# First expert layer's norm, gate, ranking and row scatter inside the attention iterations, one row for both choices

## The chip, the cores and the metric

One core of one Trainium2 chip. The metric is device time in microseconds (us) of one execution. The core has five engines with queues of their own: TensorE (PE in the profile, its weight loads PEld), VectorE (DVE), ScalarE (ACT), GpSimd (POOL) and SyncE (SP, which here only issues DMAs). Each works its queue in order; they meet through semaphores.

## The reference, cut to what matters

32 batches of 256 tokens with 128 channels go through two layers. The change touches the first, attention and a mixture of experts, both behind a norm that a condition vector scales and shifts:

```python
h = layernorm(x) * (1 + scale_a) + shift_a
c_k = h @ w_dk + b_dk; k = c_k @ w_uk + b_uk          # v likewise; q = h
q, k = rope(q), rope(k)                               # 16 heads of 8
x = x + gate_a * (softmax(q k^T / sqrt(8)) v @ w_o + b_o)

h = layernorm(x) * (1 + scale_b) + shift_b            # what is moved
logits = h @ gate_w                                   # [tokens, 8]
top_vals, top_idx = top_k(logits, 2)
mult1 = softmax over experts not masked by (thr - logits) / max(|logits|, thr) > 0.02, at top_idx[0]
mult2 = the same for the second choice, the first set to -inf
y = sum over the 8 experts of w_e * ((silu(h @ w1[e]) * (h @ w3[e])) @ w2[e])
x = x + gate_b * y
```

Each token goes to two of eight experts. The second layer (a Mamba mixer in both directions, a Fourier KAN and a one-choice mixture) follows and is not changed.

## The kernel before, in words

X, the residual, stays in SBUF: 64 tiles of 128 tokens, two per batch (TC = 2). The program is a row of stages; in each, every engine has its code written out in full, and waits on semaphores order them.

`load_and_modulate` loads constants and X. `attention` (from line 358) is one software pipeline over i = 0 to 37, unrolled. Iteration i handles six batches at different ages: projections and rotary sum of batch i, its load from DRAM in split bf16 parts (i+1), row maxima of the scores (lag MAX = 2), their transpose (ROWS = 3), scores, exponentials and values (AV = 4), sums and transposes (OUT = 5), bias, gate and residual update (LAST = 6). TensorE runs eight slots per iteration (`slot`), each with two row-maximum products (L632), one score product pair (L645) and one value product (L659); small steps stand between the slots, and all of these write the one PSUM bank `PP` (a_proj). VectorE runs 16 row maxima per iteration (`row_max`, L566) from a buffer two deep, with the other steps between them by hand; TensorE waits for the maximum before last. ScalarE runs eight exponentials (L483). GpSimd runs the gate product and update (L446, L450), the cosine product (L454), and two of the rotary split steps (L458, L461). SP stores the split parts and loads Q and K.

After the loop `norm_stats` finishes mean and deviation for all 64 tiles, `pad_rows` makes the filler rows, and `ffn_front` (line 764) runs alone: ScalarE normalises (L841) and copies each row a second time for its second choice (L835 also serves that copy and the transposed tile), VectorE modulates (L944, L946), TensorE turns (L899) and gates (L885), and VectorE routes groups of eight tiles (`route`): two times maximum, equality, rank by expert (L950 to L954), limits, weights, and slots from counts that TensorE sums with a triangular matrix and one of ones (L891, L892). GpSimd sends each row of 130 numbers (128 channels, destination row, weight) to its slot in DRAM by an indirect DMA of 128 rows: 64 tiles x 2 choices = 128 scatters (L913). At the end VectorE writes the table of expert and first row for 71 tiles of 256 slots (L1037 to L1054), and SP stores a filler block behind each expert's rows, at an address loaded from `pad_row` (L829, L830).

`experts0` (line 1057) then takes 71 tiles: SP loads rows (L1091) and weights (L1092) by the table, TensorE turns (L1112) and multiplies (L1135, L1139, L1122), VectorE takes index and weight from the row (L1175, L1176), GpSimd scatters the result (L1185).

Of the kernel before, what the change touches and what calls it, by code (L numbers as in the profile page):

```python
# [13 lines left out]
P = 128  # L14
# [122 lines left out]
def load_and_modulate(core, first):  # L137
# [3 lines left out]
    for n, shape, dt in (("bias_kv", [P, 2], F32), ("bias_cols", [P, 4], F32), ("bias_out", [P, TC * D], F32), ("bias_out_row", [1, D], F32),  # L141
                         ("b_o_row", [1, D], F32), ("ones_row", [1, P], F32), ("cos", [P, 2 * T], F32), ("sin", [P, 2 * T], F32),
                         ("minus_one", [2, H * T], BF16)):
        kept[n] = core.sbuf("a_" + n, shape, dt, on=first)
# [5 lines left out]
    w_dk, w_dv, w_uk, w_uv, w_uvg, w_o, rot, w_k, w_v, bias_kv, bias, bo, bo_row, bo_in, ones1, cos, sin, minus = (kept[n] for n in (  # L150
        "w_dk", "w_dv", "w_uk", "w_uv", "w_uv_by_group", "w_o", "rot", "w_k", "w_v", "bias_kv", "bias_cols", "bias_out", "bias_out_row", "b_o_row",
        "ones_row", "cos", "sin", "minus_one"))
    on = ExitStack()
    with on:
        c = core.sbuf("c_rows", [2 * B, D], on=on)
# [141 lines left out]
def ln_finish(core, tag, st, eps, block):  # L297

    nc = core.nc
    m, dm, v, sd = core.ln_tmp  # L300
    s_v, s_sd = core.sem(f"{tag}_var_ready"), core.sem(f"{tag}_std_ready")

    @block.vector
    def _(dve):
        chain = Chain(core, dve, f"{tag}_dve_chain")

        chain.step(nc.vector.tensor_tensor(m[:], st[:, :, 1], st[:, :, 4], ALU.add))
        nc.vector.tensor_tensor(dm[:], st[:, :, 1], st[:, :, 4], ALU.subtract)
        chain.step(nc.vector.tensor_tensor(v[:], st[:, :, 2], st[:, :, 5], ALU.add))
        chain.step(nc.vector.tensor_tensor(dm[:], dm[:], dm[:], ALU.mult))  # L310
        chain.step(nc.vector.tensor_scalar(dm[:], dm[:], 0.25, eps, ALU.mult, ALU.add))
        nc.vector.scalar_tensor_tensor(out=v[:], in0=v[:], scalar=1.0 / D, in1=dm[:],
                                       op0=ALU.mult, op1=ALU.add).then_inc(s_v, 1)
        dve.wait_ge(s_sd, 1)
        chain.step(nc.vector.reciprocal(core.rstd[:], sd[:]))
        chain.step(nc.vector.scalar_tensor_tensor(out=core.nmr[:], in0=m[:], scalar=-0.5, in1=core.rstd[:],
                                                  op0=ALU.mult, op1=ALU.mult))

    @block.scalar
    def _(act):  # L320
        act.wait_ge(s_v, 1)
        nc.scalar.activation(sd[:], v[:], ACT.Sqrt).then_inc(s_sd, 1)


# [5 lines left out]
def norm_stats(core, tag, eps=LN_EPS):  # L330

    with core.nc.Block() as block:
        ln_finish(core, tag, core.st, eps, block)

PAIRS = H // 2
# [22 lines left out]
def attention(core, kept):  # L358
    nc, B, X, aps = core.nc, core.B, core.X, core.aps
# [7 lines left out]
    valued = lambda p: ((p - 7) % PAIRS, ROWS if p == 7 else AV)  # L367
    on = ExitStack()
    with on:
# [17 lines left out]
        y1, y2 = sb("y1", [P, TC * D]), sb("y2", [P, TC * D])  # L387
        ST = core.psum("a_scores", [P, 2, 2, TC, T], on=on)
# [10 lines left out]
            "y_ps", "y_biased", "y_gated", "x_updated", "stats")}  # L399
        loaded = [core.sem(f"a_loaded{n}") for n in range(RING)]  # L400

        with nc.Block() as block:
            @block.sync
            def _(sp):
# [3 lines left out]
                for i in range(B + LAST):  # L408
# [16 lines left out]
                    if live(i, 1):  # L425
# [4 lines left out]
                        for turn in range(PARTS):  # L430
# [3 lines left out]
                            if turn:  # L434
                                sp.dma_start(K9[n][first + cut:past, :, :].rearrange("p h t -> p (h t)"), rows[1, 0:turn * DH]).then_inc(loaded[n], 16)

            @block.gpsimd
            def _(pool):
                for i in range(B + LAST):
                    if live(i, LAST):  # L440
# [9 lines left out]
                        nc.gpsimd.tensor_tensor(x, x, y2[:], ALU.add).then_inc(S["x_updated"], 1)  # L450
# [296 lines left out]


GT = 8
NB = GT // TC  # L750
PADROW = 1.0e6


# [2412 lines left out]
```

## Time and profile before

| | us |
|---|---|
| timed runs, median of 3 | 3265.21 (3264.02 to 3269.38) |
| profiled execution, span from first to last instruction (the profile gives no other time of it) | 3315.9 |
| attention, first instruction to last residual update | 0 to 617.8 |
| stage of norm, gate, ranking, scatter | 617.8 to 852.2 |
| first experts, from their first matmul | 852.2 to 1245 |

| of the span | TensorE | VectorE | ScalarE | GpSimd |
|---|---|---|---|---|
| busy us | 2742.9 | 2509.0 | 2252.2 | 2145.6 |

Busy shares over the whole span mix stages with different limits. A stage is read from the windows: which engine is busy all the time there, at which granted TensorE clock (1.00 is 2.4 GHz, 0.5 is 1.2 GHz), and what the others wait for. In timelines the bracket at the end of a row is the idle time of that engine before it, and what ended it.

### The profile page before, as it was taken

What the parts mean: (1) busy time and instruction counts of PE and PEld (TensorE: products, weight loads), DVE (VectorE), ACT (ScalarE), POOL (GpSimd) and SP (SyncE); (2) the same over time, 40 slices, a digit from 0 to 9 for tenths busy, and PEclk for the clock granted to TensorE, in tenths of its full rate; (3) what the DMA queues carried; (4) which work ended last, traced back from release to release, by engine and by line L of the source; (5) the groups of instructions that cost most, each with busy time, mean ns of one, the idle gap of its engine ahead of it and who ended that gap; (6) DMA issues with size and microseconds to landing.
All of it is one profiled execution on the core that took longest, in us unless ns stands there. A gap on an engine that the chain in (4) does not pass through costs nothing. (4 is left out here: it accounts for less than half of the span.)

```text
span 3315.9 us, 55572 instructions
## 1 busy us (share of the span) xinstructions
PE 2742.9 (83%) x18699; PEld 2096.9 (63%) x18699; DVE 2509.0 (76%) x3291; ACT 2252.2 (68%) x4086; POOL 2145.6 (65%) x1488
## 2 busy tenths in 40 slices
PE   6999999522699996788888888989888887769983
PEld 3555555311699993466666666666666666669983
DVE  5788887434233334699999999999999999967993
ACT  2677776511222224999999999999999999656651
POOL 2233332266233334899999999999999999743574
PEclk6999998655899998899999999999999999889996
DMA  5555554211566666222222222222222222322322
GB/s 134 99 102 102 101 101 82 60 58 51 160 190 193 193 178 209 81 78 78 77 73 85 80 81 80 83 74 76 84 81 80 83 77 75 102 55 72 81 73 53
DMA packets 202783, 321.54 MB, mean 97 GB/s; under 512 B 37418, under 2 KB 109638, under 8 KB 197898
## 3 DMA queue, kind: packets, MB, share of 16 engines
q1 hardware_dynamic: 189282, 299.01, 32.8%
q0 software_dynamic: 12224, 18.29, 1.6%
q8 instruction: 160, 2.62, 0.3%
q14 instruction: 109, 0.89, 0.1%
q10 hardware_dynamic: 1008, 0.72, 0.1%
HBM read 269.84 MB, written 55.68 MB: 98 GB/s over the span
## 5 line engine op out<-in xcount | busy, mean ns | idle before, releaser
L1702 POOL TENSOR_TENSOR resid_x<-s_ux,s_B_rows 128x1024 f32<-128x1024 f32 x256 | 605.3, 2364 | 85.6 <-PE s_y L2432 84.5
L2263 DVE TENSOR_TENSOR_SCAN resid_x<-s_dA,resid_x 128x1024 f32<-128x1024 f32 x256 | 581.8, 2273 | 28.9 <-ACT s_dA L1914 22.6
L2271 DVE TENSOR_TENSOR_SCAN resid_x<-s_late,s_back_in 128x1024 f32<-128x1024 f32 x256 | 583.4, 2279 | 20.8 <-ACT s_late L1924 16.4
L2432 PE MATMUL s_y<-identity,resid_x 128*128 128x128 f32 x4096 | 552.4, 279 | 10.5 <-issue 8.4
L2432 PEld LDWEIGHTS s_y<-identity,resid_x 128*128 128x128 f32 x4096 | 493.3, 145 | 65.1 <-issue 38.9
L1710 POOL TENSOR_TENSOR resid_x<-resid_x,s_C_rows 128x1024 f32<-128x1024 f32 x192 | 453.7, 2363 | 0.2 <-DVE resid_x L2263 0.2
L566 DVE TENSOR_REDUCE a_row_max<-a_maxscores 128x2 f32<-128x512 f32 x512 | 336.3, 684 | 89.2 <-PE a_maxscores L632 88.7
L2278 DVE TENSOR_TENSOR resid_x<-resid_x,s_C 128x1024 f32<-128x1024 f32 x320 | 382.1, 1194 | 5.5 <-PE s_C L2407 5.5
L1914 ACT ACTIVATE s_dA<-s_dt,s_A 128x510 f32<-128x510 f32 x512 | 330.0, 676 | 67.7 <-DVE resid_x L2263 66.5
L2419 PE MATMUL s_back_in<-identity,resid_x 128*128 128x128 f32 x2048 | 291.4, 288 | 101.3 <-ACT resid_x L1935 53.0
L1924 ACT ACTIVATE s_late<-s_dt,s_A 128x510 f32<-128x510 f32 x512 | 338.0, 710 | 0.0
L2419 PEld LDWEIGHTS s_back_in<-identity,resid_x 128*128 128x128 f32 x2048 | 239.1, 147 | 143.9 <-issue 79.1
L483 ACT ACTIVATE a_probs<-a_scores 128x1024 f32<-128x1024 f32 x256 | 262.1, 1024 | 94.7 <-PE a_scores L645 88.3
L1185 POOL DMA_INDIRECT choice_outputs<-e_y,e_idx x142 | 137.8, 971 | 273.3 <-DVE e_y L1176 249.4
L1169 DVE TENSOR_TENSOR e_g<-e_silu,e_ps 128x512 f32<-128x512 f32 x142 | 97.7, 688 | 283.4 <-PE e_ps L1139 282.2
L1158 ACT ACTIVATE e_silu<-e_ps 128x512 f32<-128x512 f32 x142 | 84.8, 597 | 242.1 <-PE e_ps L1135 240.1
L2990 PE MATMUL k_psY<-k_coef_T,k_basis 128*128 128x128 f32 x2048 | 235.5, 277 | 6.7 <-ACT k_basis L2953 4.3
L2990 PEld LDWEIGHTS k_psY<-k_coef_T,k_basis 128*128 128x128 f32 x2048 | 232.8, 194 | 7.5 <-DVE k_basis L2881 4.7
L632 PE MATMUL a_maxscores<-a_K,a_Q 72*128 72x256 bf16 x1024 | 207.8, 287 | 15.6 <-DMA a_K<-split_qk 11.3
L2459 PE MATMUL s_prep<-s_xT,k_coef_T 128*128 128x512 f32 x464 | 210.9, 596 | 2.7 <-ACT s_xT L2012 1.6
L2407 PE MATMUL s_C<-s_bc_parts,s_w_sel 96*128 96x512 bf16 x320 | 125.9, 393 | 88.5 <-DVE resid_x L2278 88.5
L913 POOL DMA_INDIRECT slot_inputs<-choice_rows,f_slots x128 | 125.9, 983 | 95.5 <-DVE f_slots L1009 57.8
(463 smaller groups left out, 5643.8 us busy)
## 6 DMA issues: line engine op xcount, KB each, us to landing
s_B_rows<-forward_rows SPq DMA_DIRECT2D x256, 256.0 KB, 3.2
e_w<-L_ffn_w_by_expert SPq DMA_DIRECT2D x71, 768.0 KB, 4.6
s_C_rows<-forward_rows SPq DMA_DIRECT2D x192, 256.0 KB, 3.3
a_Q<-split_qk SPq DMA_DIRECT2D x96, 192.0 KB
split_qk<-a_parts SPq DMA_DIRECT2D x32, 384.0 KB, 2.8
e_x<-slot_inputs SPq DMA_DIRECT2D x71, 130.0 KB
a_K<-split_qk SPq DMA_DIRECT2D x64, 128.0 KB
s_late<-choice_outputs SPq DMA_DIRECT2D x16, 512.0 KB, 4.6
```

Source lines behind the costliest of these rows:

```text
L483: nc.scalar.activation(PT[:, q % 4].rearrange("p a b t -> p (a b t)"), ST[:, q % 2].rearrange("p a b t -> p (a b t)"), ACT.Exp, scale=SCAL ...
L566: nc.vector.tensor_reduce(mx[b % 2][:, h, :], MX[:, h % 2], AX.X, ALU.max).then_inc(S["max_done"], 1)
L1702: tt(R[s, 0], ux[par][:], brow[s % BRING][:].unsqueeze(1).broadcast_to([P, C2, W]), ALU.mult).then_inc(S["in_ready"], 1)
L1710: tt(r, r, crow[k % CRING][:].unsqueeze(1).broadcast_to([P, C2, W]), ALU.mult).then_inc(S["part_pool"], 1)
L1914: last = func(dA[:, c2, :, 1:T], dt[par][:, 0, c2, :].rearrange("p (g t) -> p g t", t=T)[:, :, 1:T], ACT.Exp, scale=Wt["A"][:, 0, c2, s:s ...
L1924: last = func(dec[s % 2][:, c2, :, 0:T - 1], dt[par][:, 1, c2, :].rearrange("p (g t) -> p g t", t=T)[:, :, 0:T - 1], ACT.Exp, scale=Wt["A" ...
L2263: nc.vector.tensor_tensor_scan(r, a, r, 0.0, ALU.mult, ALU.add).then_inc(S["scanned"], 1)
L2271: nc.vector.tensor_tensor_scan(r[:, ::-1], a[:, ::-1], b[:, ::-1], 0.0, ALU.mult, ALU.add).then_inc(S["scanned"], 1)
L2278: tt(r, r, CP[:].unsqueeze(1).broadcast_to([P, C2, W]), ALU.mult).then_inc(S["part_dve"], 1)
L2419: last = nc.tensor.transpose(bP[:, c2, k // TC, (k % TC) * P:(k % TC + 1) * P], bt[s % 2][:, k, c2 * P:(c2 + 1) * P], core.ident[:])
L2432: last = mm(YP[:, t, c2 * P:(c2 + 1) * P], R[s, d][:, c2, t * P:(t + 1) * P], core.ident[:], is_transpose=True, start=((s, d) == (0, 1) an ...
L2990: last = mm(psY[:, j % 2, k * D:(k + 1) * D], basis[j % 2][:, m, k * P:(k + 1) * P], WT[:, m, :], start=(m == EARLY[0] and k == 0), stop=( ...
```

## The change

1. `ffn_front`, `norm_stats`, `ln_finish` and `pad_rows` go. `FrontPlan` lays their steps into the attention's turns: groups of four batches (five of them) and then of two (six); a batch's norm stands at least seven turns behind its last attention input; choice and ranking one and two turns after the group's last norm; scatters four per turn up to turn 31 or 32, then all that are open. The loop gets 43 turns instead of 38.
2. By FrontPlan for 32 batches: one norm per turn in turns 11 to 31 (batches 0 to 20), two in 32, 33, 35, 37 and 39, one in 34; choices in turns 15, 19, 23, 27, 31, 33, 34, 35, 36, 38, 40; rankings in 16, 20, 24, 28, 32, 34, 35, 36, 37, 39, 41; scatters: 4 in each of turns 17 to 32, 16 in 33, 8 in each of 35, 36, 37, 38, 40, 42.
3. The variance (seven small operations) and the modulation move to GpSimd, the root becomes Ln and Exp on ScalarE, the norm stays on ScalarE. Transposes, gate products and counts use free columns of `PP`. The counts become bf16 and add up over the group's tiles in PSUM (1 + 8 matmuls for eight tiles).
4. One row of 132 numbers serves both choices: it holds token row, both weights, and the rank of the first expert; both scatters of a tile read it. `experts0` finds by that rank which choice a row is (`code_of_tile`) and forms index and weight in five small VectorE operations per tile.
5. The tables are made by 16 operations on all partitions at the end of the loop. The rotary sum stays on VectorE.

```diff
+        for b in range(B):
+            i = max(self.groups[self.group_of[b]][1] + last + 1, self.norm_at[b - 1] if b else 0)
+            while held.get(i, 0) >= (2 if i >= B else 1):
+                i += 1
+            self.norm_at[b] = i
...
+                def modulate(b):
+                    g = plan.group_of[b]
...
+                    pool.wait_ge(S["f_xn"], b + 1)
+                    pool.wait_ge(S[f"f_mod_loaded{b % 2}"], 16 * (b // 2 + 1))
...
+                    gtt(h, h, row(1), ALU.mult).then_inc(S["f_scaled"], 1)
...
+                    gtt(h, h, row(0), ALU.add).then_inc(S["h_ready"], 1)
...
+                    if i in plan.root_at:
+                        offset(plan.root_at[i])
+                    if plan.early(i) is not None:
+                        modulate(plan.early(i))
+                    if plan.late(i) is not None:
+                        modulate(plan.late(i))
+                    sent, due = plan.scattered_by.get(i - 1, 0), plan.scattered_by[i]
+                    scatters(sent, (sent + due) // 2)
                     if live(i, 0):
                         pool.wait_ge(S["k_ready"], i + 1)
                         at(pool, S["roped_ready"], i)
                         nc.gpsimd.tensor_tensor(qcos[:], qk[:].rearrange("p a t -> p (a t)"), cos[:], ALU.mult).then_inc(S["cos_done"], 1)
+                    scatters((sent + due) // 2, due)
...
+                    if i in plan.rank_at:
+                        places(plan.rank_at[i])
+                    if plan.late(i - 1) is not None:
+                        logits_kept(i, plan.late(i - 1))
+                    row_max(i, 2)
+                    row_max(i, 3)
+                    if i in plan.rank_at:
+                        distances(plan.rank_at[i])
+                    row_max(i, 4)
+                    if i in plan.rank_at:
+                        slot_rows(plan.rank_at[i])
+                    row_max(i, 5)
+                    if i in plan.rank_at:
+                        limits(plan.rank_at[i])
...
+                    if i in plan.rank_at:
+                        weights(plan.rank_at[i])
...
                     row_max(i, 10)
+                    if i in plan.choose_at:
+                        first_choice(plan.choose_at[i])
                     row_max(i, 11)
...
                     row_max(i, 13)
+                    if i in plan.choose_at:
+                        second_choice(plan.choose_at[i])
...
+                    for k in range(TC):
+                        last = nc.tensor.transpose(PP[:, T + k * P:T + (k + 1) * P], Hrow[g % HRING][:, n + k, 0:D], core.ident[:])
...
+                    for k in range(TC):
+                        last = mm(PP[:, T + k * E:T + (k + 1) * E], hT[:, k, :], gw[:], start=True, stop=True)
...
+                    mm(PP[:, P:P + n * E], tri[:], flat, start=True, stop=False, skip_group_check=True)
+                    for j in range(1, n + 1):
+                        last = mm(PP[:, P + j * E:P + (n + 1) * E], allone[:], flat[:, 0:(n + 1 - j) * E], start=False, stop=(j == n), skip_group_check=True)
...
                     slot(i, 6)
...
+                    if plan.late(i) is not None:
+                        second_turn(i, plan.late(i))
```

In a norm's turn ScalarE runs the two norms after exponential 0 and the copy of the turned tiles before exponential 7; the gate product of that batch comes at the start of the next turn, after slot 0. In `experts0` the wait for earlier stores of a buffer moves half a tile forward, from the output product to the index.

## Rows read from the trace of the kernel before

**Rows 1.** Windows by stage: busy us (count) per engine, clock, DMA share, GB/s
```profile
335.00:536.00 201.00, 198.93 (x1831) 118.54 (x1826) 163.71 (x307) 148.74 (x220) 61.21 (x62) 1.00 0.53 102
562.00:590.00 28.00, 27.16 (x152) 12.97 (x153) 13.04 (x23) 10.18 (x11) 2.19 (x4) 0.52 0.02 4
852.00:1245.00 393.00, 390.69 (x2411) 356.70 (x2412) 125.97 (x282) 113.26 (x214) 133.94 (x138) 0.99 0.61 189
```
**Rows 2.** Instruction groups, the scatters: line, engine, operation, shapes, count, busy us, mean, idle
```profile
L913 POOL DMA_INDIRECT slot_inputs<-choice_rows,f_slots x128 | 125.9, 983 | 95.5 <-DVE f_slots L1009 57.8 <-issue 32.3 <-DMA slot_inputs<-choice_rows,f_slots 5.5
```
**Rows 3.** Timeline of GpSimd, one iteration: start, us, engine, line, operation, idle before
```profile
350.73 0.73 POOL L446 TENSOR_TENSOR a_y<-a_y,a_gate_rows 128x256 f32<-128x256 f32 x1 [1.22 <-DVE a_y L573]
356.77 1.28 POOL L454 TENSOR_TENSOR a_qk_cos<-a_qk,a_cos 128x512 f32<-128x512 f32 x1 [4.52 <-ACT a_qk L498]
362.23 1.15 POOL L458 TENSOR_TENSOR a_left<-a_roped,a_parts 128x512 f32<-128x512 f32 x1 [4.18 <-DVE a_roped L596]
364.75 1.16 POOL L461 TENSOR_TENSOR a_parts<-a_left,a_parts 128x512 bf16<-128x512 f32 x1 [1.37 <-ACT a_parts L519]
367.13 0.73 POOL L446 TENSOR_TENSOR a_y<-a_y,a_gate_rows 128x256 f32<-128x256 f32 x1 [1.22 <-DVE a_y L573]
```
**Rows 4.** Timeline of GpSimd, gate products and last update
```profile
547.59 0.73 POOL L446 TENSOR_TENSOR a_y<-a_y,a_gate_rows 128x256 f32<-128x256 f32 x1 [1.22 <-DVE a_y L573]
561.40 0.72 POOL L446 TENSOR_TENSOR a_y<-a_y,a_gate_rows 128x256 f32<-128x256 f32 x1 [12.29 <-DVE a_y L573]
588.58 0.73 POOL L446 TENSOR_TENSOR a_y<-a_y,a_gate_rows 128x256 f32<-128x256 f32 x1 [25.65 <-DVE a_y L573]
616.23 0.72 POOL L446 TENSOR_TENSOR a_y<-a_y,a_gate_rows 128x256 f32<-128x256 f32 x1 [4.21 <-DVE a_y L573]
617.03 0.72 POOL L450 TENSOR_TENSOR resid_x<-resid_x,a_y 128x256 f32<-128x256 f32 x1
```
**Rows 5.** Timeline of TensorE in iteration 350.73
```profile
353.23 0.44 PE L684 MATMUL a_proj<-identity,a_xn 128*128 128x128 f32 x2
353.50 0.38 PE L632 MATMUL a_maxscores<-a_K,a_Q 72*128 72x256 bf16 x2
355.58 0.61 PE L691 MATMUL a_proj<-a_w_v,a_qk 128*128 128x128 f32 x4
356.02 0.38 PE L632 MATMUL a_maxscores<-a_K,a_Q 72*128 72x256 bf16 x2
```
**Rows 6.** Timeline of VectorE, the end of that iteration
```profile
363.27 2.60 DVE L566 TENSOR_REDUCE a_row_max<-a_maxscores 128x2 f32<-128x512 f32 x4
366.63 0.43 DVE L573 TENSOR_TENSOR a_y<-a_proj,a_bias_out 128x256 f32<-128x256 f32 x1 [0.76 <-PE a_proj L720]
```
**Rows 7.** Timeline of VectorE in the ranking of the old stage
```profile
640.00 0.22 DVE L953 TENSOR_REDUCE f_rank<-f_cand 128x8 f32<-128x64 f32 x1
640.25 0.22 DVE L954 TENSOR_TENSOR f_choice<-f_cand,f_rank 128x64 f32<-128x64 f32 x1
```
**Rows 8.** Timeline of TensorE at the start of iteration 33
```profile
562.84 0.39 PE L632 MATMUL a_maxscores<-a_K,a_Q 72*128 72x256 bf16 x2 [1.98 <-DMA a_K<-split_qk]
```
**Rows 9.** Timeline of ScalarE in the old stage
```profile
632.90 0.37 ACT L835 ACTIVATE f_hT<-f_psT 128x256 f32<-128x256 f32 x1
633.16 0.87 ACT L841 ACTIVATE f_xn<-resid_x,neg_mean_rstd,rstd 128x128 f32<-128x128 f32 x2
```
**Rows 10.** Timelines and waits at the end of the old stage
```profile
838.19 0.97 POOL L913 DMA_INDIRECT slot_inputs<-choice_rows,f_slots  x1 [0.30 <-issue]
...
812.54 33.39 SPq L830 DMA_DIRECT2D slot_inputs<-f_pad_rows  x8
849.97 0.37 SPq L1091 DMA_DIRECT2D e_x<-slot_inputs  x1
...
SPq L801 <- DMA slot_inputs<-f_pad_rows: 2.0, 1, 2.0
...
852.16 0.69 PE L1112 MATMUL e_psX<-identity,e_x 128*128 128x128 f32 x2 [45.57 <-DMA e_x<-slot_inputs]
```

More of the change, by code:

```diff
@@ L294, in load_and_modulate @@
     return kept
[L297 to L322, printed above, removed]
@@ L325, in tile_stats, with region @@
 def tile_stats(core, src, tile):
     return core.nc.vector.bn_stats(core.st[:, ds(tile, 1), :].rearrange("p n k -> p (n k)"), src[:, ds(tile * D, D)])
-def norm_stats(core, tag, eps=LN_EPS):
-    with core.nc.Block() as block:
-        ln_finish(core, tag, core.st, eps, block)
 PAIRS = H // 2
+E, F = 8, 512
+FC = F // P
+STAGES = 4
+CAP = 80
+ROWS0 = 2
+TOK = ROWS0 * P
+GT = 8
+NB = GT // TC
+PADROW = 1.0e6
+HRING = 4
+ROW_TOK, ROW_W, ROW_RANK = D, D + 1, D + 3
+def region(core):
+    return core.NT * P + TOK
@@ L440, in _ @@
+                nc.gpsimd.memset(allone[:], 1.0)
+                nc.gpsimd.memset(pad[:], 0.0).then_inc(S["f_pad"], 1)
+                pool.wait_ge(S["f_pad"], 1)
+                nc.gpsimd.memset(pad[:, :, ROW_TOK], PADROW).then_inc(S["f_pad"], 1)
+                for i in range(plan.turns):
                     if live(i, LAST):
@@ L569, in _ @@
+                front_constants()
+                for i in range(plan.turns):
                     if live(i, LAST):
@@ L668, in slot @@
                     values(i, p)
-                for i in range(B + LAST):
+                for i in range(plan.turns):
+                    turned = max((b for b in plan.norm_at if plan.norm_at[b] < i), default=-1) + 1
+                    ranked = sum(1 for turn in plan.rank_at if turn <= i)
                     slot(i, 0)
+                    if plan.late(i - 1) is not None:
+                        logits(i, plan.late(i - 1))
+                    if i in plan.rank_at:
+                        counts(i, plan.rank_at[i])
                     if live(i, ROWS):
@@ L3093, in adaln_two_layers @@
     with core.stack:
+        XS, tables, tiles = choice_buffers(core)
         first = ExitStack()
         with first:
-            attention(core, load_and_modulate(core, first))
+            attention(core, load_and_modulate(core, first), XS, tables, tiles)
         late = ExitStack()
         with late:
-            YS, kept = ffn0(core, late)
+            YS, kept = ffn0(core, late, XS, tables, tiles)
             core.next_stage()
```

647 lines of the change are left out of this document (325 added, 322 removed).

## The prediction

> **What bounds the kernel now.** I read the windows by stage first, then the timelines of single engines. In a steady attention iteration (335 to 536) TensorE is busy 198.9 of 201.0 us at clock 1.00 while VectorE has 163.7, ScalarE 148.7 and GpSimd 61.2 [rows 1]: TensorE's instruction count sets the 16.40 us of an iteration (367.13 less 350.73 [rows 3]). The expert layer's norm, gate and scatter stand alone after it. The last attention update starts at 617.03 and takes 0.72 us [rows 4], so X is final at 617.75; the first expert matmul starts at 852.16 [rows 10]. That is 234.4 us with TensorE almost empty. Of it GpSimd issues 128 scatters, 125.9 us busy at 983 ns each [rows 2], and with the 0.30 us between two the pitch is 1.27 us: 163 us. So the stage is bound by GpSimd's issue of scatters, and behind it is a tail: last scatter ends 839.16, first expert load issues 849.97, first matmul 852.16 [rows 10]. From 852 on TensorE is again full, 390.7 of 393 us [rows 1].
>
> **What the change does to the end of the chain.** The stage goes; 64 scatters fall into turns 17 to 32 (4 in each), where GpSimd has 11 us free per iteration, and 64 into turns 33 to 42 (16, then 8 in each of six). So the new end is: attention up to turn 32, slower by what is added; then GpSimd's serial work from turn 33; then the old tail.
>
> *Attention, turns 11 to 31.* One batch per turn adds two transposes and two gate matmuls. A pair of such transposes advances TensorE 0.27 us (353.23 to 353.50), four f32 records with 128x128 weights 0.44 us (355.58 to 356.02) [rows 5]. 21 x 0.27 + 20 x 0.44 = 14.5 us, all on the bound engine. Counts: nine bf16 matmuls per group; the trace has no such row. From above 0.11 us each, the average over the 1831 records of 335 to 536 [rows 1], so 1.0 us; from below nothing. I take 0.6, since the columns are 64 at most: four groups, 2.4 us.
>
> *VectorE.* The ranking is cut in small operations, each awaited: pitch 0.26 us at 128x64 (640.00 to 640.25 [rows 7]). A turn that chooses gets twelve, 1.55 us between row maxima 10 and 11 and 1.55 between 13 and 14. That is where VectorE has no room: four row maxima stand back to back at 0.65 us from 363.27 to 365.87, and the only gap is the 0.76 us before 366.63 [rows 6]. TensorE's score buffer is two deep, so it stands still: about 1.2 us at the first insertion and 0.45 at the second after the added TensorE work is set against it, 1.65 in all. A turn that ranks gets twelve operations plus the logits copy, 3.4 us, but most in the first half, where there is slack; only the three before row maximum 10 hit the tight part. I take 0.9 us. From below both are zero (the 0.7 us that TensorE is longer gives VectorE room), from above the whole 3.1 and 3.4 us. Five choosing turns and four ranking turns before turn 32: 8.3 + 3.6 = 11.9 us (0 to 29).
>
> *ScalarE* gets two norms (0.87 us for the pair) and one copy (0.37 us) [rows 9] per turn, beside 52 us idle in 201 [rows 1], so 4.2 us free per iteration: covered; without the cover 1.2 us a turn, 26 us. *GpSimd*: an iteration has 0.73 + 0.72 + 1.28 + 1.15 + 1.16 = 5.0 us [rows 3]; modulating adds two of 0.73 and scatters 4 x 1.27, 11.6 us of 17.1. The halves fit the gaps: gap to the cosine product 4.5 us (modulate, two scatters: 4.0, though it waits for the norm first, perhaps 0.5 late), gap to L458 4.2 us (two scatters: 2.5). Behind GpSimd's scatter waits only the rotary chain, whose sum is needed 2 us later. Its statistics (seven small operations of about 0.2 us) come after L461 and before the next gate product; the update they delay is read 5 us later. SP gets one 128 KB load a turn behind the K/Q loads: covered, since it is last in the queue.
>
> Turn 32 began on GpSimd at 547.59 [rows 4]; now 547.6 + 14.5 + 2.4 + 11.9 = 576.4.
>
> *Turn 32 and 33.* Turn 32 took 561.40 - 547.59 = 13.8 us [rows 4]; it gets two turns of rows, two logits, counts and a ranking: + 3.0, so turn 33 starts at 593.2. Turn 33 before lasted 27.2 us (588.58 less 561.40). It starts with TensorE's 1.98 us wait for a K load [rows 8], and the window 562 to 590 has clock 0.52 [rows 1]. With turn 32 longer by 3 us that wait should go, and turn 33 should take about 14 + 2.5.
>
> *GpSimd serial from 593.2.* Turn 33: gate 1.5, two modulates 3.1, 16 scatters 20.4, statistics 2: to 620.2. Turn 34: VectorE's bn_stats stand before the row sums and wait for GpSimd's update, 620.2 + 1.5; then statistics 0.5, choice 1.3, division and product 0.8 (VectorE), transposes, copy, projection and bias 2.5: about 628. Turn 35: 1.5 + 3.1 + 8 scatters 10.2 + 2, to 645. Turn 36: 1.5 + 10.2, to 656.9. Turn 37: 1.5 + 3.1 + 10.2 + 2, to 673.7. Turn 38: root on ScalarE 1, 10.2, to 685. Turn 39: two modulates, 688.3. Turn 40: 698.5. Turn 42: 708.7. The last group's own chain (turn, gate, two choices, counts, places, weights) runs on VectorE beside turn 40 and ends near 697.5; the 16 operations for the tables then need some 7 us, to 704.5, and are hidden. Add 2.0 us for the last write to land (as the pad writes: 2.0), and 849.97 - 847.9 + 2.2 = 4.3 for block end, register loads and first load [rows 10]: first expert matmul at 715.
>
> 852.2 - 715 = 137 us of the profiled span. Two corrections. The eight pad stores, with the register loads between them, took 33.4 us (812.54 on [rows 10]) while scatters ran; the span is 3315.9 us against the 3265.2 of the timed runs, so stretches like this may be the profile's. Without it the old stage ends with the scatters, 839.2 + 2 + 4.3 = 845.5, and the saving is 130. And I allow 7 us for late K loads, since traffic rises and a single load already was late once. Saving 123 to 124.
>
> The experts get five VectorE operations of 128x2 per tile (0.17 us each at most) on an engine busy 126 of 393 us [rows 1]: nothing; without cover 71 x 0.8 = 57 us. Rows are 528 instead of 520 bytes: nothing. The write wait is now for the tile three before instead of four; those scatters lie two tiles (11 us) back.
>
> **Rivals.**
> *Clock lost in a few turns.* Speaks for it: one wait of 1.98 us was followed by 27 us at 1.2 GHz, although TensorE was then busy 27.16 of 28 us [rows 1, 8]: at the lower level this loop doesn't win the clock back by itself. My choosing turns have stalls of 1.2 us. Against: the rows show no case between an undisturbed iteration and the 1.98 us, so I can't place the point; and transposes and gate matmuls are added. Each loss costs 27.2 - 13.8 = 13.4 us: one to five of them, 3155 to 3208.
> The Trainium skill, page TensorE: Matmul & The Clock Gate (Part 1: The HAM clock gate), says that the throttled state is the default and recent activity releases it. The trace agrees that the lower level follows a stretch with little work, and differs in the return: TensorE was dense for 27 us and stayed at 1.2 GHz. If activity released it at once, a loss would cost a few us instead of the 13.4 that the row gives, and the sum would be 3141 with or without losses.
> *The clock lost for good, slower than before.* The same, but from turn 15 to 31: an iteration of 16.4 + 0.7 us becomes twice (27.2 / 13.8 = 1.97) as long, + 16.6 us each, 17 turns 282 us, less the 12 us of stalls that then hide: 3141 + 270 = 3411. It decides the sign from 124 / 16.6 = 7.5 such turns on.
> *Scatters don't fit between GpSimd's rotary steps.* Each turn with scatters would be longer by up to 4 x 1.27 = 5.1 us, 16 turns: + 82, 3223. For: the first gap is 4.5 us and 4.0 plus a wait for ScalarE goes in. Against: the product has 2 us of slack.
> *VectorE absorbs all and the waits in turn 34 vanish.* 12 + 8 + 7 us better: 3114.
>
> **How the numbers follow.** Forecast 0.60; a few clock losses 0.20; scatters don't fit 0.09; absorbed 0.06; clock lost for good 0.05. Time 3265.2 - 124 = 3141 us. Range 3112 to 3200: it takes in the absorbed case, the upper bound of the VectorE stalls (+17), uncovered K loads, and the cases of one to four clock losses; above it are the fifth loss, most of the misfit case and the last rival. A run can't tell less than 0.2% (6.5 us) from no change. Faster 0.94, same 0.01, slower 0.05.
>
> **What would show it.** Distance of two GpSimd gate products: about 17.1 us in plain turns, 18 to 19 in turns 19, 20, 23, 24; first e_psX matmul near 715; TensorE waits on row maxima of about 1.2 us in choosing turns; no K wait in turn 33 and clock 1.00 until about 610; scatters back to back at 1.27 us from turn 33. Wrong would be: a clock of 0.5 in the loop, GpSimd's cosine product later than 2 us, or a stage between the last scatter and the experts longer than 10 us.

## The result, and the profile after

| | us |
|---|---|
| timed runs, changed kernel, median of 4 | 3225.89 (3214.50 to 3238.96) |
| the kernel before beside them, median of 4 | 3267.14 (3264.02 to 3269.38) |
| ratio | 0.9864, 95% interval 0.9829 to 0.9899 |
| profiled execution: span / its own time | 3221.9 / 3223.75 |
| first expert matmul | 761.7 (before 852.2) |

The kernel is 41 us faster, a third of the 124 us predicted, and outside the range of 3112 to 3200 us. Each of the two kernels was profiled again, unchanged, and the comparison below needs these profiles too.

**The loop.** Windows of the changed kernel: turns 15 and 16 (the first that chooses and the first that ranks), a plain turn, turn 33, what follows it, and the experts; the last figures are the granted clock, DMA share and GB/s. They answer to [rows 1].

```profile
core 0: us, PE busy (x) PEld busy (x) DVE busy (x) ACT busy (x) POOL busy (x), PEclk, DMA share, GB/s
270.00:291.00 21.00, 19.03 (x152) 11.26 (x145) 16.48 (x39) 13.21 (x21) 6.35 (x9) 0.86 0.47 96
291.00:314.00 23.00, 22.59 (x168) 13.09 (x167) 15.84 (x39) 13.37 (x22) 6.34 (x8) 0.76 0.41 64
331.00:348.00 17.00, 17.00 (x159) 10.45 (x158) 13.34 (x26) 13.47 (x23) 10.87 (x13) 1.00 0.60 119
624.00:652.00 28.00, 19.27 (x197) 11.33 (x194) 16.76 (x50) 12.78 (x20) 21.80 (x31) 0.91 0.17 53
652.00:762.00 110.00, 42.67 (x235) 23.00 (x235) 34.32 (x164) 23.89 (x48) 66.81 (x90) 0.50 0.16 50
762.00:1155.00 393.00, 390.68 (x2414) 357.28 (x2412) 159.23 (x567) 113.26 (x214) 134.02 (x138) 0.99 0.62 190
```

A plain turn is full and at 1.00. The choosing turn has TensorE 19.0 of 21 us busy, and the clock is down to 0.86 in it and to 0.76 in the next one, where TensorE is busy 22.6 of 23 us for work that fits in 17.5 at full clock. The predicted sign of a wrong forecast, "a clock of 0.5 in the loop", is there: TensorE runs at 1.2 GHz for 17.1 us from 285.1, and again from 363.6, 445.6, 524.1 and 602.6, once in each of the five choosing turns. Just ahead of every one stands the same row, here TensorE in turns 15 and 23 (the bracket is the idle time before the row and what ended it; it answers to [rows 5]):

```profile
284.35 0.39 PE L970 MATMUL a_maxscores<-a_K,a_Q 72*128 72x256 bf16 x2 [1.97 <-DVE a_row_max L770]
...
444.15 0.39 PE L970 MATMUL a_maxscores<-a_K,a_Q 72*128 72x256 bf16 x2 [1.97 <-DVE a_row_max L770]
```

**VectorE and GpSimd ahead of that wait** (timelines of turn 15; before, this place looked as in [rows 6]):

```profile
280.63 0.69 DVE L770 TENSOR_REDUCE a_row_max<-a_maxscores 128x2 f32<-128x512 f32 x1
281.23 0.21 DVE L802 TENSOR_REDUCE a_top<-a_biased 128x8 f32<-128x64 f32 x1
281.48 0.23 DVE L803 TENSOR_TENSOR a_is_max<-a_biased,a_top 128x64 f32<-128x64 f32 x1
281.74 1.06 DVE L804 TENSOR_TENSOR a_cand<-a_is_max,a_rev 128x64 f32<-128x64 f32 x1
282.83 0.22 DVE L805 TENSOR_REDUCE a_choice_rows<-a_cand 128x8 f32<-128x64 f32 x1
283.09 0.23 DVE L806 TENSOR_TENSOR a_choice<-a_cand,a_choice_rows 128x64 f32<-128x64 f32 x1
283.35 0.23 DVE L807 SCALAR_TENSOR_TENSOR a_biased<-a_choice,a_biased 128x64 f32<-128x64 f32 x1
283.61 0.69 DVE L770 TENSOR_REDUCE a_row_max<-a_maxscores 128x2 f32<-128x512 f32 x1
```

```profile
281.51 1.20 POOL L613 TENSOR_TENSOR a_left<-a_roped,a_parts 128x512 f32<-128x512 f32 x1 [4.18 <-DVE a_roped L926]
```

The six operations of the first choice were to take 1.55 us between the row maxima. They take 2.38, and the surplus is one operation: L804, 1.06 us where its neighbours of 128x64 take 0.23. It begins after GpSimd's difference L613 (281.51 to 282.71) and ends just behind it, at 282.80.

**The drain.** GpSimd in turns 33 to 35 and at the end, TensorE's first expert row, and all scatters as one group (these answer to [rows 2, 3, 10]):

```profile
629.69 1.04 POOL L575 DMA_INDIRECT slot_inputs<-a_choice_rows,a_slots  x1 [0.16 <-POOL a_choice_rows L563]
...
648.92 0.97 POOL L575 DMA_INDIRECT slot_inputs<-a_choice_rows,a_slots  x1 [0.30 <-issue]
...
651.54 0.72 POOL L591 TENSOR_TENSOR a_y<-a_y,a_gate_rows 128x256 f32<-128x256 f32 x1
...
653.98 0.72 POOL L563 TENSOR_TENSOR a_choice_rows<-a_choice_rows,a_mod_rows_b 128x256 f32<-128x256 f32 x1
667.00 0.73 POOL L591 TENSOR_TENSOR a_y<-a_y,a_gate_rows 128x256 f32<-128x256 f32 x1 [12.30 <-DVE a_y L889]
```

```profile
752.29 0.97 POOL L575 DMA_INDIRECT slot_inputs<-a_choice_rows,a_slots  x1 [0.30 <-issue]
```

```profile
761.66 0.69 PE L1193 MATMUL e_psX<-identity,e_x 128*128 128x128 f32 x2 [27.11 <-DMA e_x<-slot_inputs]
```

```profile
L575 POOL DMA_INDIRECT slot_inputs<-a_choice_rows,a_slots x128 | 127.7, 998 | 40.5 <-issue 36.9 <-DVE a_choice_rows L856 2.6 <-POOL a_choice_rows L563 0.9
```

Turn 33 (gate product to gate product) is 27.05 us, as predicted: its 16 scatters follow each other at 1.27 us. Then GpSimd stands idle for 12.3 us, until VectorE's bias step for the next update is done. VectorE had itself stood for 9.37 us behind GpSimd's update L595, which follows the scatters:

```profile
653.16 0.49 DVE L299 BATCH_NORM_STATS2 bn_stats<-resid_x 128x6 f32<-128x128 f32 x2 [9.37 <-POOL resid_x L595]
```

From 646.9 us on TensorE runs at 1.2 GHz for the whole rest of the drain. In the second profile of the changed kernel (e11 below) it runs so for 13.7 us from 638.5 and then at 2.4 GHz for 17 us, and there GpSimd's wait in turn 34 is 9.60 us (e11):

```profile
656.41 0.73 POOL L591 TENSOR_TENSOR a_y<-a_y,a_gate_rows 128x256 f32<-128x256 f32 x1 [9.60 <-DVE a_y L889]
```

**The kernel before, profiled twice more** (c0 and c1 below). Windows of c0: turn 33 and the old stage; under it the same two stretches of c1.

```profile
558.00:574.00 16.00, 14.55 (x147) 8.64 (x151) 12.65 (x24) 9.03 (x11) 1.46 (x3) 1.00 0.03 8
602.00:803.00 201.00, 48.91 (x224) 45.19 (x224) 95.91 (x433) 50.38 (x139) 126.42 (x128) 0.50 0.26 76
```

```profile
561.00:588.00 27.00, 25.07 (x147) 12.52 (x151) 13.35 (x24) 9.16 (x10) 1.79 (x3) 0.57 0.02 5
616.00:817.00 201.00, 48.91 (x224) 45.18 (x224) 95.92 (x433) 50.38 (x139) 126.49 (x129) 0.50 0.25 76
```

The stage that I had priced at 234.4 us is 201 in both, with equal busy times. The first expert matmul is at 803.2 and 817.3, not 852.2. In the first profile GpSimd had three gaps that the others do not have (8.97, 10.10 and 9.96 us; the first is shown, from the kernel before). And SP's eight pad stores took 8.18 us in c1 instead of 33.39 [rows 10]; from the end of the last scatter to the issue of the first expert load it was 10.8 us in the first profile and 5.3 us in c0 and c1.

```profile
696.54 1.17 POOL L913 DMA_INDIRECT slot_inputs<-choice_rows,f_slots  x1 [8.97 <-DVE f_slots L1009]
```

```profile
736.31 8.18 SPq L830 DMA_DIRECT2D slot_inputs<-f_pad_rows  x8
```

### The profile page after: what moved, and what is told of

Same layout as the page of the kernel before. It is cut to its first block and busy times, and to the rows that moved or that the text cites. A ratio compares the mean times of both kernels' runs of the same rounds, so it can differ in the third digit from the quotient of the medians.

```text
span 3221.9 us, 56259 instructions
## 1 busy us (share of the span) xinstructions
PE 2767.1 (86%) x18742; PEld 2103.5 (65%) x18742; DVE 2513.1 (78%) x3462; ACT 2241.6 (70%) x4076; POOL 2212.7 (69%) x1654
## 5 line engine op out<-in xcount | busy, mean ns | idle before, releaser
L2508 PE MATMUL s_y<-identity,resid_x 128*128 128x128 f32 x4096 | 560.6, 282 | 11.7 <-issue 10.5
L2508 PEld LDWEIGHTS s_y<-identity,resid_x 128*128 128x128 f32 x4096 | 500.5, 147 | 68.1 <-issue 43.2
L2011 ACT ACTIVATE resid_x<-s_uT,s_bT 128x256 f32<-128x256 f32 x432 | 185.3, 498 | 0.8
```

Source lines behind the costliest of these rows:

```text
L2508: last = mm(YP[:, t, c2 * P:(c2 + 1) * P], R[s, d][:, c2, t * P:(t + 1) * P], core.ident[:], is_transpose=True, start=((s, d) == (0, 1) an ...
```

## Experiments

Times are compared through the ratio to the kernel before on the same chip, where there is one.

**c0_before_again, c1_before_again: the kernel before, unchanged.**

> The kernel before, unchanged, profiled once more. Its first profile spans 3315.9 us against 3265 in timed runs, and it shows two things that need not repeat: 27.3 us of half clock from 563 and 31 us of SyncE and VectorE issuing one instruction per 0.7 to 1.4 us from 812 on. Theory A (the profile's own disturbance): the span falls to within 15 us of 3267 and at least one of the two is gone. Rival (both belong to the kernel): span again above 3300 with both.

> The kernel before once more, unchanged. The first profile had a stage of 234 us between attention and experts and a turn 33 of 27.2 us, the second 201 us and 15.7 us. If the first was disturbed in the stage, this one has 200 to 205 us there; turn 33 may be either (the wait for the K load was 1.98 us where the clock fell and 1.74 us where it stayed).

3262.12 and 3281.77 us, first expert matmul 803.2 and 817.3. The stage is 201.2 and 201.3 us. Turn 33 is 15.7 us in c0 and 26.2 in c1, and this is what lies ahead of it on TensorE (c0, then c1):

```profile
559.45 0.39 PE L632 MATMUL a_maxscores<-a_K,a_Q 72*128 72x256 bf16 x2 [1.74 <-DMA a_K<-split_qk]
```

```profile
562.93 0.39 PE L632 MATMUL a_maxscores<-a_K,a_Q 72*128 72x256 bf16 x2 [2.04 <-DMA a_K<-split_qk]
```

So the first profile was longer by 33 us in the stage, by 11.5 in turn 33 compared with c0, and by 3.3 ahead of turn 6. The stage's 33 us are in neither of the other two executions; turn 33's clock is lost in c1 as it was in the first. What made the stage longer stays open.

**e1_spread: the changed kernel, its choices cut up.** In turns before 34 the twelve choice operations go one to three at a time behind row maxima 3, 5, 6, 7, 9, 11, 13, 15, and the last three of a ranking go behind 9, 10, 11.

```diff
+AFTER = {3: 1, 5: 3, 6: 1, 7: 2, 9: 1, 11: 1, 13: 1, 15: 2}
...
 row_max(i, 10)
-first_choice(plan.choose_at[i])       # six awaited operations
 row_max(i, 11)
+take(choosing, AFTER[11])             # one
```

> The changed kernel with the twelve operations of both choices laid singly or in pairs and threes into VectorE's gaps between row maxima (1 after maximum 3, 3 after 5, 1 after 6, 2 after 7, 1 after 9, 11 and 13, 2 after 15) in turns 15, 19, 23, 27, 31 and 33, and the three weight operations after 9, 10, 11. Theory (TensorE's stall of over 1 us costs the clock): no half clock in turns 15 to 32, those turn pairs fall from 44 to 47 us to about 36, turn 32 starts near 570 instead of 608, time about 3187 (3175 to 3200). Rival 1 (the clock falls for the number of VectorE operations or the DMA load, not for the stall's length): clock losses stay, within 8 us of 3226. Rival 2 (gain is eaten by GpSimd in the drain): turn 32 starts near 570, but the first expert matmul moves less than 15 us.

3181.16 us (3178.35 to 3183.01), ratio 0.9721 (0.9697 to 0.9744). Windows of turns 15 and 16, and TensorE's longest wait in them:

```profile
270.00:289.00 19.00, 17.70 (x166) 10.33 (x164) 17.43 (x40) 13.75 (x22) 7.11 (x9) 1.00 0.57 112
289.00:306.00 17.00, 16.91 (x163) 10.16 (x156) 14.99 (x38) 12.97 (x22) 5.97 (x8) 1.00 0.51 92
```

```profile
285.04 0.44 PE L1052 MATMUL a_proj<-identity,a_choice_rows 128*128 128x128 f32 x2 [0.66 <-DVE a_out_rows L987]
```

No clock is lost in turns 6 to 32; the first expert matmul is at 717.7. Theory and size hold: this placement alone is worth 44 us at the first expert matmul. TensorE's wait in the other four choosing turns is 0.67 us. The hold behind GpSimd's difference is not gone: the third choice operation, L823 at 283.22, still takes 0.92 us. But it now stands alone, and TensorE waits 0.66 us for it instead of 1.97 for all six.

**e3_filler: the changed kernel, with TensorE kept busy.** VectorE's work stays as it is; TensorE repeats score products (same result) in slots 6 and 7 of choosing turns.

```diff
+for turn in range(1 + extra):         # extra: 2 in slot 6, 1 in slot 7
     for j, h in enumerate(pair_heads(q)):
```

> The changed kernel with added work: in the choosing turns TensorE repeats the score product of slot 6 twice and that of slot 7 once (same values written again), so that it works where it stood still for VectorE. Theory (the clock falls because TensorE does too little in the stall): although 12 matmuls per choosing turn are added, no half clock in turns 15 to 31, pairs of turns about 37.5 us, time 3190 to 3205. Rival (lost time is the stall itself, or the clock falls for another reason): time 3226 or up to 7 us more, half clock as before.

3200.53 us (3187.87 to 3213.24), ratio 0.9792 (0.9752 to 0.9831). The longest wait is 1.10 us, the clock falls in one of the five turns (I had expected none), and turn 15 takes 19.7 us instead of 21.3. VectorE's operations are all still there, and yet the first expert matmul is at 726.3, 35 of e1's 44 us earlier; by the ratios it is 24 of 47 us, the runs falling into two groups (3187.9 to 3190.1 and 3211.0 to 3213.2). So half of the loss or more was the clock and not VectorE's time.

**e4_stall_before: the kernel before, with the stall alone.** Six awaited operations of 128x64 on a scratch tile at the two places, in turns 15, 19, 23, 27, 31.

```diff
 row_max(i, 10)
+if i in (15, 19, 23, 27, 31): idle_ops()   # a fill and five products
 row_max(i, 11)
```

> The kernel before with nothing of the change but six awaited operations on a small scratch tile (128x64) on VectorE after row maxima 10 and 13 of turns 15, 19, 23, 27 and 31. Theory (a stall of 1.2 us is enough to lose the clock, and in this loop it comes back only after 17 to 24 us): five stretches at half clock, about 8 to 10 us each: 3267 + 40 to 55 us = 3307 to 3322. Rival (a stall costs its own length): 1.65 to 3.1 us each, 3275 to 3283, clock 1.00 from 120 to 540.

3323.45 us (3312.05 to 3333.53), ratio 1.0143 (1.0110 to 1.0175): 51 us slower than the kernel before on the same chip, within the 40 to 55 expected. VectorE, GpSimd and TensorE in turn 15:

```profile
280.36 2.10 DVE L558 TENSOR_TENSOR a_dummy<-a_dummy 128x64 f32<-128x64 f32 x5
...
285.21 1.26 DVE L558 TENSOR_TENSOR a_dummy<-a_dummy 128x64 f32<-128x64 f32 x5
```

```profile
280.44 1.15 POOL L458 TENSOR_TENSOR a_left<-a_roped,a_parts 128x512 f32<-128x512 f32 x1 [4.18 <-DVE a_roped L603]
```

```profile
283.24 0.39 PE L643 MATMUL a_maxscores<-a_K,a_Q 72*128 72x256 bf16 x2 [1.93 <-DVE a_row_max L573]
```

Five products take 1.26 us at the second place and 2.10 at the first, where GpSimd's difference runs. All five turns lose the clock. The losses are not alike: the first four have 13.7 to 17.1 us of half clock and cost 8 to 10 us each with the wait itself, the one of turn 31 takes 61.4 us, through turns 32 and 33, which are 25.4 us each instead of the 13.8 and 15.7 of c0.

**e7_half_stall, e10_three_again, e8_stall_four, e9_stall_five: how long the wait is.** As e4, with three, three again, four and five operations.

```diff
-for _ in range(6):
+for _ in range(3):                    # e7 and e10; 4 in e8, 5 in e9
```

> The kernel before with three awaited scratch operations instead of six at each of the two places, in the same five turns (15, 19, 23, 27, 31). Theory A: the loss of the clock has a point between the stalls that kept it (1.10 us) and those that lost it (1.93 us), and this one stays below it with about 1.1 us: no half-clock stretch in those turns, choosing turns 17.2 to 17.8 us, 4 to 8 us slower than before in all. Theory B: the clock already falls at stalls of this length in this loop: choosing turns near 19 and the next near 21, 35 to 50 us slower than before.

> The kernel before with four scratch operations at each of the two places in turns 15, 19, 23, 27, 31. Three gave TensorE a wait of 1.15 us in each of the five turns, and the clock fell in two of them; six gave 1.93 us and it fell in all five. Theory A, the longer the wait the more often it falls: a wait near 1.4 us, three or four of five lost, 3295 to 3320. Theory B, the length in this range doesn't matter and other things decide (then the five of five at 1.93 us were chance): one or two lost.

> As the run before it with five scratch operations: a wait near 1.65 us. Theory A: four or five of five lost, 3305 to 3330. Theory B: again one or two.

> The kernel with three scratch operations once more, unchanged, since the same wait of 1.15 us had kept the clock in turns 15, 19 and 27 and lost it in 23 and 31. If it is a matter of chance between executions, other turns lose it now, one to three of five; if something in turns 23 and 31 decides, the same two: 3295 to 3312 either way.

| | wait in each of the five turns, us | turns that lost the clock | time, us |
|---|---|---|---|
| e7 | 1.15 | 2 (23, 31) | 3303.06 (3300.65 to 3311.74), ratio 1.0097 (1.0066 to 1.0128) |
| e10 | 1.15 | 2 (19, 27) | 3293.16, one run |
| e8 | 1.41 | 3 | 3315.65, one run |
| e9 | 1.67 | 5 | 3331.76, one run |
| e4 | 1.93 | 5 | 3323.45 |

e7's TensorE in turn 19, which kept the clock, and in turn 23, which lost it, and the windows of turns 16 and 24 behind such waits:

```profile
347.05 0.39 PE L643 MATMUL a_maxscores<-a_K,a_Q 72*128 72x256 bf16 x2 [1.15 <-DVE a_row_max L573]
...
413.90 0.39 PE L643 MATMUL a_maxscores<-a_K,a_Q 72*128 72x256 bf16 x2 [1.15 <-DVE a_row_max L573]
```

```profile
284.00:301.00 17.00, 16.83 (x158) 10.01 (x157) 13.99 (x27) 12.28 (x19) 5.33 (x6) 1.00 0.48 88
419.00:441.00 22.00, 21.83 (x159) 12.16 (x161) 14.07 (x27) 12.36 (x19) 5.36 (x6) 0.76 0.35 65
```

The same wait of 1.15 us has both outcomes in one execution, and the turns change between executions. My theory of a point between 1.10 and 1.93 us, with 1.15 below it, fell with e7, which is 34 us slower than before where I had 4 to 8. Most of that is the loss at turn 31, which again took in turns 32 and 33 (58.0 us at half clock in e7, e8 and e9). e10 kept the clock in turn 31 and is 2 us below its range, and e9 is 2 us above its own. The counts 2, 2, 3, 5, 5 of five rise with the wait, but e12 below breaks the row.

**e11_after_again: the changed kernel, unchanged.**

> The changed kernel once more, unchanged. Its first profile lost the clock in all five choosing turns at a wait of 1.97 us, 9 to 10 us each. Expected again in four or five of five, 3213 to 3240, and the first expert matmul between 755 and 775 us; if the losses of the first profile were chance, one to three, 3190 to 3210 and 725 to 745 us.

3215.63 us, first expert matmul 749.4. Three turns lose the clock (15, 19, 27), as in my second case, and 23 and 31 keep it at the same wait; the time is in the range of my first case and the matmul between the two, for I had put a loss at 9 to 10 us. TensorE in turns 15 and 23, and the windows of the turns behind them:

```profile
285.82 0.39 PE L970 MATMUL a_maxscores<-a_K,a_Q 72*128 72x256 bf16 x2 [1.98 <-DVE a_row_max L770]
...
444.65 0.39 PE L970 MATMUL a_maxscores<-a_K,a_Q 72*128 72x256 bf16 x2 [1.98 <-DVE a_row_max L770]
```

```profile
292.00:316.00 24.00, 23.59 (x174) 13.62 (x176) 16.57 (x41) 13.82 (x23) 6.98 (x8) 0.75 0.40 67
450.00:467.00 17.00, 16.59 (x162) 10.25 (x155) 15.11 (x39) 12.92 (x22) 10.10 (x11) 1.00 0.56 102
```

Turns 15 and 16 take 21.1 + 23.4 us, turns 23 and 24 take 19.7 + 17.5: one loss costs 7.3 us here, 8.8 in turns 19 and 20. So the number of losses can account for a part of the spread of the changed kernel's runs, 3214.5 to 3239.0; how many losses the runs without a profile had isn't shown.

**e12_one_input, e13_left_written_only: who holds VectorE.** e12 is e4 with reductions in place of the five products. In e13, the changed kernel, GpSimd's L613 writes zeros instead of reading two tiles; this leaves out the second and third part of the rotary split, so e13 computes something else and serves as a test alone.

```diff
-tt(dummy[:], dummy[:], dummy[:], ALU.mult)                            # e4
+nc.vector.tensor_reduce(dummy2[:], dummy[:], AX.X, ALU.max)           # e12
```

```diff
-nc.gpsimd.tensor_tensor(left[:]..., roped[:]..., parts[:, :, 0, :], ALU.subtract).then_inc(S["left1"], 1)
+nc.gpsimd.memset(left[:], 0.0).then_inc(S["left1"], 1)                # e13
```

> The kernel before with the six scratch operations of e4 at the same places, but as a fill and five reductions of 128x64 to 128x8 (one input tile each) instead of products (two input reads each). In e4 the five products took 2.10 us after row maximum 10, where GpSimd's difference (128x512, 1.15 us, at 280.44) ran beside them, and 1.26 us after row maximum 13, where GpSimd was idle: 0.84 us of the 1.93 us wait. Theory A, VectorE's products and GpSimd's difference can't run at the same time and a reduction can: 1.26 us at both places, TensorE's wait near 1.1 us, two of five turns with a lost clock, 3290 to 3305. Theory B, something else holds VectorE there (the semaphore steps, the row maximum's buffer): the wait stays 1.9 us, five lost, near 3323. By the Trainium skill, page SBUF — State Buffer, a VectorE instruction with two inputs in SBUF blocks against a GpSimd instruction that reads SBUF, one with a single input does not; by that rule theory A.

> The changed kernel, in which GpSimd fills the residue of the rotary split with zeros (it writes only) in place of the difference that reads two tiles; this leaves out the second and third part of that split. Theory A: the third operation of the first choice (1.06 us at 281.74, its like 0.23) goes back to 0.23, TensorE's wait in choosing turns from 1.97 to about 1.15 us, the clock is lost in two or three of five turns, 3190 to 3212. Theory B: the operation is long for another reason, 1.97 us and four or five lost, 3214 to 3239.

VectorE, GpSimd and TensorE of e12 in turn 15 (this execution's turns start 8 us later than e4's); the last row is from turn 23:

```profile
287.87 1.24 DVE L558 TENSOR_REDUCE a_dummy<-a_dummy 128x8 f32<-128x64 f32 x5
...
291.86 1.24 DVE L558 TENSOR_REDUCE a_dummy<-a_dummy 128x8 f32<-128x64 f32 x5
```

```profile
287.96 1.16 POOL L458 TENSOR_TENSOR a_left<-a_roped,a_parts 128x512 f32<-128x512 f32 x1 [4.18 <-DVE a_roped L603]
```

```profile
289.89 0.39 PE L643 MATMUL a_maxscores<-a_K,a_Q 72*128 72x256 bf16 x2 [1.06 <-DVE a_row_max L573]
...
441.62 0.38 PE L643 MATMUL a_maxscores<-a_K,a_Q 72*128 72x256 bf16 x2 [0.49 <-DVE a_row_max L573]
```

VectorE's third operation of the first choice in e13, and TensorE's wait in turn 19:

```profile
278.36 0.22 DVE L803 TENSOR_TENSOR a_cand<-a_is_max,a_rev 128x64 f32<-128x64 f32 x1
```

```profile
350.21 0.39 PE L969 MATMUL a_maxscores<-a_K,a_Q 72*128 72x256 bf16 x2 [1.13 <-DVE a_row_max L769]
```

Both say theory A for the held operation: reductions take 1.24 us at both places though GpSimd's difference runs from 287.96 to 289.12, and the operation of 1.06 us is 0.22 once GpSimd does not read. The Trainium skill, page SBUF — State Buffer (Who interferes with whom), says that a VectorE instruction with two inputs in SBUF contends with a GpSimd instruction that reads SBUF. The trace agrees, with 0.84 us (1.06 less 0.22 in e13, 2.10 less 1.26 in e4).

On the clock they differ. e13: 3189.24 us (3184.42 to 3193.47), ratio 0.9736 (0.9663 to 0.9809), wait 1.13 us, no loss in five turns, first expert matmul 715.8; a little better than I had it. e12: 3315.06 us (3302.62 to 3334.37), ratio 1.0120 (1.0044 to 1.0195); with a wait of 1.06 us its profiled execution lost the clock in four of five turns, which I had not expected (I had two, and 3290 to 3305 us). So the shortest wait lost the clock more often than e7's and e10's 1.15 us, and the wait's length is not all. e12 has a second, shorter wait after row maximum 13 (0.49 us in turn 23, the one that kept the clock), e13 has one of 0.39 to 0.42 us in every choosing turn and lost nothing, and in e12's four losses the clock was down within 2.1 us of the end of the first wait, about 2 us before the place of the second; so it isn't the second wait. With waits of 1.06 to 1.15 us the variants of the kernel before (e7, e10, e12) lost it in 8 of 15 turns, those of the changed kernel (e3, e13) in 1 of 10. The counts are small. The two kernels differ in what TensorE does around the wait; whether that matters, and which part of it, wasn't tried.

**e5_paced: e1 with at most eight scatters per turn in the drain.**

```diff
-            sent = open_rows if i >= B else min(open_rows, sent + 4)
+            sent = min(open_rows, sent + (4 if i < B else 8))
```

> The spread choices of e1, and from turn 33 on at most 8 scatters per turn instead of all that are open (turn 33 had 16, turn 34 none). Theory A: turn 33 was as long as GpSimd's 16 scatters (20.4 us at a pitch of 1.27), and GpSimd then stood idle for 9.6 us in turn 34 while TensorE and VectorE caught up. Paced, eight of them fill that idle time: turn 33 near 17 us, turn 34 near 15, the first expert matmul 7 to 10 us earlier than e1's 717.7, time 3171 to 3175 on the scale of e1's 3181. Theory B: turn 34's idle time is the length of the chain through TensorE and VectorE and only moves to another turn: 3178 to 3184.

3168.65 us (3167.51 to 3170.28), ratio 0.9684 (0.9652 to 0.9716). The first expert matmul is at 706.3, 11.4 us before e1's. Turn 33 takes 17.0 us and turn 34 13.4. The window is turn 33, in e1 27 us with TensorE busy for 18.8 of them:

```profile
582.00:599.00 17.00, 17.00 (x171) 10.40 (x170) 14.54 (x38) 11.91 (x17) 13.19 (x21) 1.00 0.16 50
```

Theory A, a little more than its range. It beats both kernels.

**e6_pool_delay: e1 with GpSimd delayed in turns 36 and 38.**

```diff
+if i in (36, 38):
+    for _ in range(8): chain.step(...)    # 128x256 on a scratch tile
```

> The spread choices of e1, and GpSimd has eight awaited operations of 128x256 on a scratch tile (about 0.8 us each, the first 0.4) ahead of its scatters in turns 36 and 38: 6 us of additional GpSimd time in each. Theory A, the stretch from turn 35 on is GpSimd's own work in a row: all of turn 36's 6 us and of turn 38's what the two later waits for VectorE (2.6 and 1.9 us) don't absorb, 8 to 12 us later than e1: 3189 to 3193. Theory B, the groups' chain through VectorE, TensorE and ScalarE sets the end: within 4 us of e1, 3181 to 3185.

Turn 36 grows from 11.9 to 17.9 us. Counted from turn 6, the first expert matmul is at 607.1 us against e1's 596.8: 10.3 us later, theory A. The timed median, 3197.25 us (3186.48 to 3199.45), ratio 0.9773 (0.9741 to 0.9806), is 16 us above e1's and 4 us over my range. The profiled run was the fastest of e6's five, 8 us above e1's profiled run; what the other four have beyond that stays open. B is out: from turn 36 on, GpSimd's own row of work sets the end of the drain.

## Why the prediction was wrong, point by point

**The time of what goes away was read from a disturbed profile: 46 us of the miss.** My sum began with "852.2 - 715 = 137 us of the profiled span". I saw that the span (3315.9) stood 50.7 us above the timed runs and took 6.7 us off, for the pad stores only (c0 and c1 put them at 5.5: 10.8 less 5.3). The two first profiles differ by 94.0 us in span, the timed runs by 41.3. The surplus of 52.7, less my 6.7, is this term. Two further profiles show where it was: three GpSimd gaps (29 us) and the pad stores in the stage (201 us, not 234.4), and turn 33's clock, which I took for a fixed part of the kernel.

**The loop: the rival "clock lost in a few turns" came true, and I gave it 0.20.** From turn 6's gate product to turn 32's before took 426.5 us (121.1 to 547.6); I had 28.8 more, the changed kernel has 61.3 more (120.2 to 608.0). Without a loss the pattern of four turns is 19.7 + 17.5 + 17.3 + 16.4 = 70.9 us (e11, turns 23 to 26); my terms give 18.75 + 18.0 + 17.1 + 17.1 = 70.95. So the operations were priced right in sum, with two errors that cancel: the added TensorE work is 0.46 us in a plain turn (mean of 17.3 and 16.4, less 16.40), not 0.71; and the wait at the first choice was 1.97 us, not "about 1.2". Its missing 0.8 us is VectorE's product standing still behind GpSimd's difference. In the loop that is the step that failed: with this hold removed (e13) the same turns waited 1.13 us and kept the clock, and turns 6 to 31 took 39.6 us less. That 1.2 us would always have kept it isn't shown, for e3 lost it once in five at 1.10 us. The five losses cost about 34 us in all (turns 15, 16, 19, 20, 23, 24, 27, 28 took 182.2 us, 4 x 37.2 = 148.8 without a loss, and 1.0 in turn 31).

**The rival's count was right and its price wrong.** I wrote that "at the lower level this loop doesn't win the clock back by itself" and took 13.4 us, from turn 33 of before. In the changed kernel it came back after 17 to 24 us in the first four, which cost 7.2, 10.1, 7.3 and 8.9 us, and after 3.4 in the fifth, which cost 1. At turn 31 of the variants of the kernel before, though, each of the five losses (e4, e7, e8, e9, e12) lasted 58 to 61 us. So turn 33 wasn't wrong as a row, but it is not like the turns up to 28; why the length differs by place isn't shown. The other price that I had set beside it, a few us if activity released the clock at once, is as far off on the other side. The Trainium skill, page TensorE: Matmul & The Clock Gate (Part 1: The HAM clock gate), says that activity releases the throttle. The trace agrees that TensorE's clock came back while it worked, but only after those 17 to 24 us, in which it was busy almost all the time (22.59 of 23 us in turn 16).

**GpSimd in the loop fits,** as forecast: four scatters a turn at 0.97 to 1.1 us each, the cosine product starts 6.50 us behind the gate product (e11, turn 23) instead of 6.04 [rows 3], and plain turns are as long as TensorE's work. "Scatters don't fit" is out.

**The drain** took 153.7 us from turn 32's start (608.0) to the first expert matmul; I had 138.6.

| | predicted | measured |
|---|---|---|
| turn 32 | 16.8 | 16.5 |
| turn 33 | 27.0 | 27.0 |
| turn 34 | 7.8 | 15.5 |
| turn 35 | 17.0 | 18.5 |
| turn 36 | 11.9 | 11.9 |
| turn 37 to the first expert matmul | 58.1 | 64.3 |

The serial GpSimd chain was right, tested by e5 and e6. Wrong was turn 34: I let GpSimd wait 4.6 us for a short tail (7.8 less 3.2 of its own work; the terms that I listed for the turn add up to 6.6, not 7.8) and it waited 12.3: work of TensorE and VectorE that had stood behind the held update came only then. A part of it is the clock again. In e11 and e1, where TensorE gets back to 2.4 GHz during turn 34, turn 34 is 12.8 us and turn 35 is 16.7; so 2.7 and 1.7 us of the drain's 15 come with the half clock of the first profile, and turn 35 was forecast rightly but for that. e5 shows it from the other side: with eight scatters moved from turn 33 to 34, turn 33 is 10.0 us shorter and turn 34 only 0.6 us longer. The last stretch was longer by VectorE's ranking of the tenth of eleven groups (two GpSimd waits of 2.6 and 1.9 us, in e1 as in the changed kernel) and by 2.1 us between last scatter and first matmul (8.4, not 6.3).

**Nothing for the experts' added VectorE work:** right. It is busy 159.2 us instead of 126.0, and the stretch is 393 us as before. ScalarE's added norms cost nothing either.

The miss of 83 us is then: 46 from the profile of before, 32.5 from the loop (61.3 less 28.8) and 15 from the drain, less the 7 us that I had allowed for late K loads: 86.5. The remaining 4 us are no more than single profiles and medians differ by.

## What to carry to other kernels

Before a stage's length goes into a sum, compare the span with the timed runs; where it is longer by more than they scatter, look for gaps in the stage that its own queue doesn't explain, or take a second profile. Small operations put into a full loop cost what they make the bound engine wait, and in this loop a wait of 1.06 us or more could cost the clock on top: lay them one or two at a time into gaps, away from the other engine's reads. Work that is drained after a loop is to be paced, so that its burst doesn't stand ahead of the update that the next turn needs.

## What the runs showed of the hardware that I had not expected

- The same TensorE wait in the same place has two outcomes: at 1.15 us the clock fell in 4 of 10 turns, at 1.97 us (the changed kernel, two profiles) in 8 of 10, at 0.66 us (e1, e5, e6) in none of fifteen. At 1.06 us (e12) it fell in 4 of 5, and behind a wait of 1.74 us for a K load (c0) it stayed.
- A lost clock came back by itself in the loop after 7 to 24 us. Lost in turn 31, it came back after 58 to 61 us in all five cases of the kernel before's variants and after 3.4 us in both cases of the changed kernel (first profile and e3).
- VectorE's 128x64 product takes 1.06 us instead of 0.23 when it starts under GpSimd's 128x512 difference; a reduction of the same tile doesn't notice it (five in 1.24 us at both places of e12).
- One profiled execution of the kernel before had 33 us in a stage that two others didn't have, though the busy times of VectorE, ScalarE and GpSimd differ by 1 us at most and TensorE's by 2.5.
